# Turning and normalising the attention heads on VectorE and GpSimd in a kernel of linear attention with experts, and a new order of its queues

## The reference

```python
q, k, v = xn @ Wq.T, xn @ Wk.T, xn @ Wv.T          # 16 heads of 16 features
qf, kf = taylor_exp(q), taylor_exp(k)              # so that qf.kf = 1 + s + s*s/2, s = q.k / 4
A = tril(einsum('bhnd,bhmd->bhnm', qf, kf))
y = einsum('bhnm,bhme->bhne', A, v)
z = 1.0 / (einsum('bhld,bhld->bhl', qf, cumsum(kf, axis=2)) + EPS)
y = (y * z) @ Wo.T
top_w, top_i = top_k(xn @ Wg, 2); top_w = softmax(top_w)          # 8 experts
out = sum over the two chosen e of top_w * ((silu(xn @ W1[e]) * (xn @ W2[e])) @ W3[e])
```

## Time and profile before

| | us |
|---|---|
| median of 3 runs | 632.79 (631.39 to 638.67) |
| the profiled execution's own time | 631.28 |
| its span, first to last instruction | 629.5 |
| first scores (L1223) start | 20.4 |
| last attend (L1242) starts | 292.7 |
| first expert matmul (L1372) starts | 300.2 |
| busy in the span: PE, DVE, ACT, POOL | 599.8, 467.4, 334.1, 359.7 |

### The profile page before, as it was taken

The page is one execution under the profiler, slowest core; times in us unless marked ns, Lnnn a source line. Parts: engine busy times, 40 slices in busy tenths (PEclk is TensorE's granted clock), DMA queues, the critical chain, the costliest instruction groups (busy, mean ns, idle before and its releaser), DMA issues.

```text
span 629.5 us, 16824 instructions
## 1 busy us (share of the span) xinstructions
PE 599.8 (95%) x5063; PEld 467.2 (74%) x5063; DVE 467.4 (74%) x1193; ACT 334.1 (53%) x483; POOL 359.7 (57%) x453
## 2 busy tenths in 40 slices
PE   8899999999999999998999899999999999999994
PEld 8665666767666666665788688888888888887884
DVE  6877878787878676588797477777777777777772
ACT  3668878787878677765564232333333323323331
POOL 4256463737364654557068456566666566666655
PEclk9999999999999999999999999999999999999998
DMA  4653554546544444553953567877777777777763
GB/s 134 173 130 104 124 173 108 162 104 163 125 103 124 96 130 102 160 146 104 360 112 60 126 144 159 159 160 153 156 151 157 157 142 160 153 152 150 165 119 43
DMA packets 107333, 88.13 MB, mean 140 GB/s; under 512 B 46352, under 2 KB 95376, under 8 KB 107248
## 3 DMA queue, kind: packets, MB, share of 16 engines
q1 hardware_dynamic: 73136, 54.59, 33.8%
q0 software_dynamic: 16704, 28.12, 23.3%
q10 hardware_dynamic: 17408, 4.33, 3.2%
HBM read 27.72 MB, written 22.95 MB: 80 GB/s over the span
## 4 chain that ended last, share of the span: by engine, by line
PE 48%; SPq 20%; DVE 13%; issue 9%; DMA 5%; POOL 3%; ACT 2%; POOLq 1%; DVEq 0%; ACTq 0%
SPq L481 13%; PE banks L1372 11%; PE banks L1242 10%; SPq L363 7%; PE banks L1223 6%; PE banks L1262 6%; PE banks L1271 4%; PE banks L1393 4%; DMA out<-yo,xw 2%; PE banks L1306 2%; PE banks L1291 1%; DVE yw L861 1%; PE banks L1332 1%; DMA xq<-xg 1%; POOL xg L592 1%
## 5 line engine op out<-in xcount | busy, mean ns | idle before, releaser
L618 POOL DMA_INDIRECT out<-yo,xw x71 | 112.6, 1585 | 46.1 <-DVE yo L1160 33.3
L564 POOL TENSOR_SCALAR_AFFINE_SELECT T<-T 128x512 f32<-128x512 f32 x128 | 81.0, 643 | 100.7 <-ACT T L655 48.7
L1372 PE MATMUL banks<-w12h,xgh 128*128 x284 | 114.0, 401 | 6.1 <-ACT xgh L747 5.3
L592 POOL DMA_INDIRECT xg<-xs_scr,glist x71 | 72.7, 1024 | 81.0 <-DMA xq<-xg 60.8
L774 ACT ACTIVATE hs<-banks 128x512 f32<-128x512 f32 x71 | 42.4, 598 | 142.3 <-DMA hq<-hs 67.8
L1372 PE MATMUL banks<-w12h,xgl 128*128 x284 | 113.0, 398 | 0.6 <-DVE xgl L1132 0.5
L1372 PE MATMUL banks<-w12l,xgh 128*128 x284 | 111.2, 392 | 0.0
L655 ACT ACTIVATE T<-banks 128x1024 f32<-128x1024 f32 x64 | 62.1, 1023 | 29.9 <-PE banks L1223 28.4
L559 POOL DMA_INDIRECT xs_scr<-xb,slots x64 | 63.6, 993 | 20.5 <-issue 12.4
L1242 PE MATMUL banks<-T,vau 128*17 128x512 f32 (+3 forms) x1024 | 75.2, 434 | 0.0
L1176 DVE TENSOR_TENSOR hs<-banks,hs 128x512 f32<-128x512 f32 x71 | 48.9, 689 | 30.9 <-PE banks L1372 24.9
(11 more groups left out here) (187 smaller groups left out, 1230.9 us busy)
## 6 DMA issues: line engine op xcount, KB each, us to landing
hq<-hs SPq DMA_DIRECT2D x244, 64.0 KB
w12r<-w SPq DMA_DIRECT2D x16, 512.0 KB, 5.6
Q<-Q SPq DMA_DIRECT2D x126, 64.0 KB, 2.4
out<-xa SPq DMA_DIRECT2D x16, 256.0 KB
w3r<-w SPq DMA_DIRECT2D x8, 512.0 KB, 7.7
K<-Kt SPq DMA_DIRECT2D x126, 32.0 KB
xq<-xg SPq DMA_DIRECT2D x118, 32.0 KB
xq<-xg ACTq DMA_DIRECT2D x118, 32.0 KB
```

Source lines behind the costliest of these rows:

```text
L564: e.affine_select(out=v, in_=v, pattern=[[0, 4], [1, P]], compare_op=ALU.is_ge, fill=-1.0, base=0, channel_multiplier=-1).then_inc(s["g_mk ...
L592: e.indirect_dma_start(xg[:, t % GR, :], None, xs_d, bass.IndirectOffsetOnAxis(glist[:, t:t + 1].bitcast(U32), 0)).then_inc(s[f"d_g{t % GR ...
L618: e.indirect_dma_start(out, bass.IndirectOffsetOnAxis(xw[:, t % XR, NE:NE + 1].bitcast(U32), 0), yo[:, t % 2, :], None, compute_op=ALU.add ...
L1372: i = e.matmul(banks[:, 2 * (t % 2) + m, :], a[:, k, :], w[:, bass.ds(expert[t] * 4 + (2 * k + m), 1), :], start=(k == 0 and n == 0), stop ...
```

## The change

- VectorE turns `yw` itself, by 32x32 blocks (`rows_of`): the add of CT, a transpose of 128x512 into `yt`, the reciprocal of its 16 denominators. The epsilon is now added with CT (`eps`). A head's 17 rows stand in a block of 32, so the blocks come out as tokens x (head, token block), and no full transpose is needed; rows of Wo are ordered to suit.
- GpSimd multiplies `yt` by the reciprocals into `yn` (`normalise(n - 1)`, in the masks of quad n; the last one stands ahead of the first gather).
- VectorE turns two quads of `yn` back by blocks into `yT` (`heads_of`), ScalarE rounds it (`y_high`), VectorE takes the remainder (`y_low`), both from SBUF. Steps `t` and `y` are gone from TensorE, which waits for `v_yl` before `o`.
- The order of every queue of a batch is written anew: the slots, ScalarE's and VectorE's lists, the sends of GpSimd, the W12 halves by table, the moves of SyncE (q then k of h 0, then of h 1).

```diff
-W12_WITH = {(1, 1): 0, (1, 2): 1, (2, 1): 2, (2, 2): 3, (3, 1): 4, (3, 2): 5, (4, 1): 6, (4, 2): 7, (7, 0): 8}
-W12_LOW_WITH = {(1, 2): 0, (1, 3): 1, (2, 2): 2, (2, 3): 3, (3, 2): 4, (3, 3): 5, (4, 2): 6, (4, 3): 7}
+W12_WITH = {(1, 2): 0, (2, 2): 1, (2, 3): 2, (3, 2): 3, (4, 2): 4, (4, 3): 5, (5, 2): 6, (6, 2): 7, (7, 0): 8}
+W12_LOW_WITH = {(1, 3): 0, (2, 3): 1, (3, 3): 2, (4, 3): 3, (5, 3): 4, (6, 3): 5, (7, 0): 6, (7, 1): 7}
 # slot_a
+    if qd == 0:
+        return [("C", b, 0)]
     return [("x", b + 1, 0), ("x", b + 1, 1)] if qd == 1 and 0 < b < LAST else []
 # slot_b
+    if qd == 0:
+        return [("T", b, 0), ("c", b, 2), ("r", b, 0)] if b else [("T", 0, 0), ("c", 0, 3)]
+    if b == LAST:
+        return [("f", n, 4), ("G", 0, 0)] if qd == 3 else [("f", n, 8)]
+    if qd < 3:
+        return [("c", b + 1, qd - 1), ("v", b + 1, qd - 1)]
+    return [("v", b + 1, 3)] + ([("o", b - 1, 1)] if b else [("f", n, 4)])
 # slot_c
+    if qd == 0:
+        return [("c", b, 3)]
+    if qd == 2:
+        return ([("o", b - 1, 0)] if b else [("f", n, 4)]) + ([("v", b + 1, 2)] if b < LAST else [])
+    return [("o", b - 1, 1)] if n == NQ - 1 else []
...
 # SyncE
                 for h in range(2):
                     move_q(e, b, 1, h)
-                for h in range(2):
                     move_k(e, b, 1, h)
...
 # GpSimd
+            def normalise(n):
+                b, qd = divmod(n, 4)
+                g = qd // 2
+                y = yt[n % 2].rearrange("p (k c) -> p k c", c=32)
+                e.wait_ge(s["v_rd"], n + 1)
+                if b:
+                    e.wait_ge(s["v_yb"], 2 * (b - 1) + g + 1)
+                e.tensor_tensor(yn[:, g, :, 16 * (qd % 2):16 * (qd % 2) + 16], y[:, :, 0:16],
+                                rd[:, n % 2].unsqueeze(2).to_broadcast([P, 16, 16]), ALU.mult).then_inc(s["g_yn"], 1)
 # masks, batches before the last:
 #   quad 0: T0, T1, T1, normalise, T2, T2
 #   quad 1: T0, T1, T1, normalise, send 0
 #   quad 2: send 1, T0, normalise, T1, T1, send 2, T2, T2, send 3
 #   quad 3: send 4, T0, send 5, T1, T1, send 6 and 7, normalise, root
...
 # VectorE
+            def rows_of(n):
+                e.wait_ge(s["p_av"], n + 1)
+                if n:
+                    e.wait_ge(s["v_yt"], n)
+                done(e, "T", n // 4, 0)
+                e.tensor_tensor(yw..., banks[:, 4, :]..., CT..., ALU.add).then_inc(s["v_yw"], 1)
+                e.wait_ge(s["v_yw"], n + 1)
+                if n >= 2:
+                    e.wait_ge(s["g_yn"], n - 1)
+                e.transpose(yt[n % 2][:], yw[:]).then_inc(s["v_yt"], 1)
+                e.wait_ge(s["v_yt"], n + 1)
+                e.reciprocal(rd[:, n % 2], yt[n % 2]...[:, :, 16]).then_inc(s["v_rd"], 1)
+            def heads_of(b, g):
+                e.wait_ge(s["g_yn"], 4 * b + 2 * g + 2)
+                if 2 * b + g:
+                    e.wait_ge(s["v_yl"], 2 * b + g)
+                e.transpose(yT[:], yn[:, g]...).then_inc(s["v_yb"], 1)
...
 # TensorE, step "o"
-                    for j in range(2):
-                        done(e, "y", b, j)
+                    e.wait_ge(s["v_yl"], 2 * b + 2)
```

More of the change, by code:

```diff
@@ L196, in build @@
         change = rh.take("change", 72)
+        yT = rh.take("yT", 512)
         rq = Region(344, Q1)
@@ L236, in build @@
         ry = Region(Q1, Q1 + 1024)
-        yw = [ry.take(f"yw{u}", 512) for u in range(2)]
+        yw = ry.take("yw", 512)
+        yt = [Region(at_hq + 1024, at_hq + 1536).take("yt0", 512), ry.take("yt1", 512)]
         rr = w3_hi(6, 8)
@@ L581, in masks @@
                     mask(n, T2[:, :, 256:384], 2)
-                if sends_after(n, 3):
-                    send(*sends_after(n, 3))
+                if qd == 1:
+                    send(b, *((2, 3) if late else (0, 1)))
+                elif qd == 2:
+                    send(b, *((5, 7) if late else (3, 4)))
+                elif qd == 3 and b < NBATCH - 2:
+                    root(b + 2)
             def gather(t):
@@ L623, in gpsimd_program @@
                 masks(n)
+            normalise(NQ - 1)
             done(e, "G", 0, 0)
@@ L1054, in before_b @@
                     both(0)
-                elif qd == 0:
+                    step("T", 0, 0)
+                    step("c", 0, 3)
+                    gates(0)
+                    w_low(3, Wol, wo_r, Woh)
+                    return
+                rows_of(4 * b - 1)
+                step("T", b, 0)
+                if b < LAST:
+                    rsqrt(b + 1)
+                    norm_x(b + 1)
+                step("c", b, 2)
+                places(b)
+                if b == LAST:
+                    place_rows(b)
@@ new lines, in third_quad @@
+            def third_quad(b):
+                if b == LAST:
+                    rows_of(4 * b + 1)
+                    tile_rows(0)
+                    tile_rows(1)
+                    y_low(b - 1, 1)
+                    heads_of(b, 0)
+                    all_rows()
+                    step("o", b - 1, 0)
+                    w12_low(8)
+                    return
+                step("c", b + 1, 0)
+                rows_of(4 * b + 1)
+                if b:
+                    y_low(b - 1, 1)
+                step("v", b + 1, 0)
+                heads_of(b, 0)
+                step("c", b + 1, 1)
+                step("v", b + 1, 1)
@@ new lines, in fourth_quad @@
+            def fourth_quad(b):
+                if b == LAST:
+                    rows_of(4 * b + 2)
+                    expert_ends()
+                    step("G", 0, 0)
+                    experts()
+                    step("o", b - 1, 1)
+                    return
+                if b < NBATCH - 2:
+                    sums(b + 2)
+                if b:
+                    step("o", b - 1, 0)
+                step("v", b + 1, 2)
+                if b < NBATCH - 2:
+                    variance(b + 2)
+                rows_of(4 * b + 2)
+                step("v", b + 1, 3)
+                top(b + 1, 0)
+                if b:
+                    step("o", b - 1, 1)
+                top(b + 1, 1)
+                both(b + 1)
@@ L1127, in vector_program @@
-            copy_yw(NQ - 1)
-            step("t", LAST, 3)
+            rows_of(NQ - 1)
+            y_low(LAST, 0)
             def expert_x(t):
```

267 lines of the change are left out of this document (99 added, 168 removed).

## The result

The changed kernel is slower: 666.9 us in the median (665.22 to 678.44) against 634.2 of the kernel before on the same chip, ratio 1.0516 with the 95% interval [1.0466, 1.0565]. The prediction was 627.0, faster by 0.9%, with a range of 615 to 640. On three other chips the same two kernels stand at 641 to 644 against 628 us (ratios 1.0196, 1.0207, 1.0204). So 13 to 16 of the 33 us lost come again everywhere, and the rest belongs to the first chip. The profiled execution of the changed kernel took 678.44 us, 11.5 above the median, and is the one slow execution of the five, so its rows tell where time stands and not how much the change costs.

What follows compares the result with a forecast made beforehand. TensorE was taken as the bound (29.7 of 30 us busy), with VectorE close to its limit after the change. From 631.28 us, -17.4 + 5.9 + 2.1 + 2.6 + 1.0 gave 625.5, or 627.0 in the median's terms; range 615 to 640.

Steps and rivals of the forecast that it cites:

- TensorE's 25.4 us removed: Attention stage: six transpose steps a batch leave TensorE, 3.2 us a batch, 25.4 over eight batches.
- The prices on VectorE and GpSimd: Attention stage: a 128x512 transpose on VectorE taken as 0.72 us, a normalisation on GpSimd as 0.9 us.
- The walk of the batch, P = 32.3: Middle batches: engine orders walked to get a batch's length P, 32.3 us, 2.1 less than now.
- y low: VectorE's low-half subtraction, now from two SBUF tiles: two priced at 1.3 us, placed behind the Q remainder of c(b,2).
- the chain to the remainder of c(b,2): Middle batches: VectorE runs 13.1 us without pause after attend, ending 24.9 us into the batch, before Q and K moves.
- The waits of TensorE that I named as signs: Middle batches: third quad's part 0 scores waiting on a K move, or c on xTl, by some 2 us.
- Rival 2: Attention stage: VectorE saturates, its two-input SBUF instructions waiting while GpSimd works; batch 34.9 us gives 640 us; chance 0.15.
- the prediction's formula: Whole kernel: gain is 6.7 + 5 x (34.43 - P) - 11.6 us, P being a batch's length.
- Rival 4: Attention stage: bank holders served no earlier, TensorE waits in each second quad; batch 32.9, end 3 us worse, 632; chance 0.12.
- The first batch, 5.0 gained: First batch: K moved second comes about 2 us earlier and transpose steps go, so quad 6 starts 5.0 us earlier.
- The last batch and the entry, 5.9 + 2.1 + 2.6 + 1.0 lost: Last batch: 5.9 us waiting for y low, 2.1 for the clock; entry to experts: 2.6, and 1.0 for the clock.
- The clock: Last batch and experts' entry: TensorE's idle gaps lower its clock, costing 3.1 us; without it the sum is 622.4.

Runs made afterwards that it cites:

- t1_before_again: The kernel before, unaltered, profiled again on a chip of the later runs: 628.79 us.
- s1_ylow_ahead: Changed kernel, with VectorE's low halves of the heads ahead of rows_of(4b+1) in the third quad of middle batches: 635.64 us, 1.0118 of the kernel before.
- r5_after_again: The changed kernel, unaltered, run again on another chip: 644.21 us, 1.0196 of the kernel before.
- e4_norm_vector: Changed kernel, with the normalisation on VectorE right behind the reciprocal instead of on GpSimd: 635.8 us, 1.0163 of the kernel before.
- s3_together: Changed kernel, normalisation on VectorE, low halves earlier, c(0,3) first in batch 0, last batch's heads before tile_gaps and tile_rows, W12 halves moved: 622.3 us, 0.9897.
- t2_after_fourth: The changed kernel, unaltered, run a fourth time: 640.79 us, 1.0204 of the kernel before.
- the experiments under theory A: GpSimd's sends spread apart in the changed kernel, 649.38 us (1.0376); sends packed together in the kernel before, 634.39 us (1.0132).
- the three repetitions: The changed kernel, unaltered, run again three times beside the kernel before: 644.21, 641.42 and 640.79 us (1.0196, 1.0207, 1.0204).

## Why the prediction was wrong

- **TensorE's 25.4 us removed:** right in kind, priced too high. The 24 matmuls a batch are gone. From S0(6) to S0(26) TensorE's busy time falls from 169.1 us (t1_before_again) to 156.6 (s1_ylow_ahead, where the clock doesn't fall), so by 2.5 us a batch and not 3.2. In r5_after_again it is 158.4, in a stretch as long as before: what was removed became idle time.
- **The prices on VectorE and GpSimd:** right or too high, as above. But they were prices of instructions undisturbed.
- **The walk of the batch, P = 32.3:** this failed, in two terms of it. First, y low was priced at 0.65 and stood off the path; in the three profiles it took 2.67 us or more in three, three and two of the five batches from S0(6) to S0(26), and each time kept TensorE from o for 1.4 to 1.6 us. With these waits P is 34.6, 34.6 and 33.9; without them it is 33.15 (s1), still 0.85 more than predicted. Second, the chain to the remainder of c(b,2): predicted 24.9 us after S0(4b+2), in s1 it ends at 164.0 - 137.4 = 26.6. Five small instructions on it take 0.52 to 0.68 us instead of 0.16 to 0.19, 2.0 more. Four of them end 0.01 to 0.05 us behind a mask or a normalisation (the fifth ends 0.07 behind a send); three of these, and GpSimd's, in s1_ylow_ahead:

```profile
156.05 0.58 DVE L965 TENSOR_TENSOR gx<-m 128x4 f32<-128x4 f32 x1
...
159.53 0.52 DVE L856 SCALAR_TENSOR_TENSOR sm<-sm 128x4 f32<-128x4 f32 x1
160.08 0.56 DVE L857 TENSOR_TENSOR sm<-sm 128x4 f32<-128x4 f32 x1
...
155.96 0.64 POOL L556 TENSOR_TENSOR yn<-yt,rd 128x256 f32<-128x256 f32 x1
...
158.82 1.22 POOL L545 TENSOR_SCALAR_AFFINE_SELECT T<-T 128x512 f32<-128x512 f32 x2 [0.43 <-ACT T L665]
160.00 0.62 POOL L556 TENSOR_TENSOR yn<-yt,rd 128x256 f32<-128x256 f32 x1
```

In e4_norm_vector and s3_together, where GpSimd has no normalisation, four of the five take 0.16 to 0.19 again in nearly all middle batches and the fifth (L856) 0.44, and the first of the five batches of s3_together, with no wait over 0.7 us and no fall of the clock, lasts 32.5 us. The waits of TensorE that I named as signs, at S0(4b+2) and for xTl, came: 0.3 and 1.25 us, where some 2 was said.
- **Rival 2** names this mechanism, two-input work of VectorE standing still while GpSimd works, with its break-even at P = 33.4 and 640 us at P = 34.9. Measured, (243.58 - 70.69) / 5 = 34.6 (33.9 in t2_after_fourth), and 641 to 644 us. That the times nearly agree is in part luck: by the prediction's formula P = 34.6 loses 6 us, and the rest of the 13 to 16 lost is the gain of the first batch and of S0(26) to S0(28), which didn't come. I gave it 0.15 although the row it rests on (0.19 or 0.64 for the same multiply) stood in the trace, and y low was named in it. It should have been walked: which GpSimd row stands beside the new subtraction. (Rival 4's own sum, 0.25 us lost on 631.28, gives 633 in the median's terms, not the 632 written; nothing hangs on it.)
- **The first batch, 5.0 gained:** failed. I saw the moves of K earlier and not that ScalarE's new list puts the eviction of c(0,3) behind squares2(0). Put back, S0(0) to S0(6) gains 3.7 to 4.8 on the changed kernel, and is 3.1 shorter than in the kernel before, where 5.0 was said.
- **The last batch and the entry, 5.9 + 2.1 + 2.6 + 1.0 lost:** the sum is right, 12.4 against 11.6 (9.2 to the end of attend(31), where 8.0 was said, and 3.2 behind it, where 3.6 was). TensorE's idle time in quad 30 was 8.4 us, as said, but in two waits, not one: the wait of ScalarE for the turned half had been overlooked.
- **The first chip:** 14.9 us lost in its five middle batches, where the others show from 2.7 gained to 0.7 lost, and 12.2 behind the start of the experts in its profiled execution. The prediction has no step for signals that come late, and no run tells their cause: the experiments under theory A and the three repetitions only tell that the order of the sends alone doesn't make them.
- **The clock:** "TensorE: Matmul & The Clock Gate", section "HAM oscillation" of the Trainium skill, says that idle gaps throttle it again. The trace agrees: in r5_after_again it is at the lower level 31.2 to 34.6, 113.1 to 116.5, 287.2 to 297.4 and 311.0 to 317.9, each in or right behind a gap of TensorE (2.9, 1.6, 4.0 and 4.3 us); in t1_before_again only once ahead of the end, for 3.4 us, behind a gap of 1.7 (in the expert stage, where none was expected). Not every such gap does it: three others of 1.6 us in r5_after_again (ahead of 149.2, 217.1 and 251.9) were followed by none.

## What to carry to other kernels

An operation whose operands move from PSUM to SBUF must be walked again against what GpSimd does in the same microseconds, not priced by its mean: here one subtraction of 0.7 us, begun just behind the first of four instructions of GpSimd, cost 1.6 us of the critical engine, and exchanging two lines of the order took that back. A reordering of all queues is judged by each engine's list, ScalarE's too, in the first and the last round of the loop, where the neighbours differ: a handful of exchanges, with the normalisation back on VectorE, turned +2.0% into -1.0%; with it on GpSimd they gave -0.25%, not told apart from nothing. And a ratio measured on one chip should be measured again on another.

## What the runs showed of the hardware

- VectorE's subtraction with both operands in SBUF made no headway during back-to-back GpSimd masks and a normalisation, when it began behind the start of the first of them (nine of ten cases in quads 10 to 26): 2.67 to 2.85 us instead of 0.69, ending 0.54 to 0.56 us behind the last. When it began first it took 0.72 to 0.82, and GpSimd's mask was the longer one, 1.02 to 1.04 us instead of 0.64.
- The Trainium skill, "GPSIMD Engine Reference", section "Performance versus the Vector engine", gives two-input elementwise work as about twice VectorE's time, from which the prediction estimated 0.85 us for the normalisation. It took 0.64 on GpSimd; the same from SBUF on VectorE, in e4_norm_vector, took 0.56 on the mean and 0.42 at the least. So the factor was 1.1 to 1.5.
- GpSimd's issue of a send did not do that to the same subtraction: in s1_ylow_ahead it took 0.69 at 107.61, beside a send from 106.92 to 107.99. The small instruction that ends 0.07 us behind a send there (0.68 us, at 155.34) took 0.19 in s3_together beside a send with no normalisation behind it; what made it long isn't shown.
- On one chip, ScalarE and VectorE waited 65 us in the attention stage for late signals (19 waits, the longest 5.2 us), beside sends in a row. On four others, with the same program or close kin of it, no such wait was seen.
